# Embedding tower for 512 samples: a fourth fetch of table rows moves from GpSimd's gathers to single-row DMAs of SyncE and ScalarE

## The chip, the cores and the metric

One core of a Trainium2 chip. The metric is device time in microseconds (us) of one execution; the profile is of one execution, whose span begins with the first instruction.

## The reference

For each of 512 samples, 32 rows of 256 floats are looked up in 32 embedding tables (1000, 1250 or 12500 rows each), all dot products between different rows of a sample are taken, and a small MLP follows. Cut to what matters:

```python
e = jnp.stack([tbl_0[ids[:, 0]], ..., tbl_31[ids[:, 31]]], axis=1)   # 512 x 32 x 256
iu, ju = jnp.triu_indices(32, k=1)
z = jnp.einsum('bnd,bmd->bnm', e, e)[:, iu, ju]                       # 496 dots a sample
h = jnp.concatenate([z, dense_ctx], axis=1)                           # 16 dense inputs more
h = jnp.maximum(h @ W_top1 + b_top1, 0.0)                             # 512
h = jnp.maximum(h @ W_top2 + b_top2, 0.0)                             # 256
y = h @ W_top3                                                        # 1
```

All of it is float32.

## The kernel before

**Fetches.** A fetch brings 128 table rows of 1 KB, one for each partition: four samples by 32 fields (or 28 own fields and shared places for the others). There are 120 fetches, numbered 0 to 119 and taken in 60 pairs. Blocks of 128 samples have 32, 28, 28 and 32 fetches: in the two middle blocks, four fields of small tables are not fetched but looked up on TensorE with one-hot masks (`look_up`, L460 to L475, the products of L471; its eight units are copied out by ScalarE at L842, `copy_looked_up`).

**Three ways of fetching.** 117 fetches are indirect DMAs of GpSimd (`POOL` in the profile, L402), each into one of ten buffers (`rows`, `RING`); number n of this list waits until the fetch that held its buffer is transposed (L401). The three fetches in `SINGLE` (43, 83 and 109, L75) have a buffer of their own (`single_rows`) and are fetched row by row, 384 DMAs of 1 KB. The addresses of these rows are computed by VectorE in `row_at` (L654, L657). An engine that issues rows first loads 32 addresses into registers (one TENSOR_LOAD, L364) and then issues 32 DMAs (L369), inside `fetch_rows`. SyncE does nothing else between its first loads and the last store: it issues rows 0 to 319 in order as fast as it can (L379 to L381), that is fetch 43, fetch 83 and 64 rows of fetch 109. ScalarE issues rows 320 to 383 at the end of its program for each of the pairs 10 to 41, two rows a pair (`some_rows`, L832).

**TensorE.** For each pair p (L608 to L615): transposes both fetches of pair p (`transpose_fetch`, L420; the last fetch at L624), then takes the dots of pair p-1 (`gram_pair`, L435), then a part of a look-up, then pieces of the MLP (`MLP_AT`, L501, L578, L590) or, for the last block, of the MLP by sets of 32 samples (`SETS_AT`, L520, L530, L551). The order is written out by hand in these tables. After pair 58's turn come the dots of pair 58, the transposes of pair 59, its dots and the last two sets.

**VectorE** copies each transposed pair from PSUM (L337, L340), makes the masks (L672) and copies half of the dots to `z` (L321, L328). **ScalarE** copies the other half. In its turn for pair p it does, in this order: the MLP's activations, `copy_looked_up` if a unit ended with pair p-1, `place(p+1)` (L354: it puts the looked-up rows of pair p+1 beside the fetched ones, for which `gram_pair(p+1)` waits), dots, a piece of `move_dots` (L805: four small DMAs within SBUF for each block, which the first MLP product of the block waits for; those of block 0 in pairs 20 to 23, of block 1 in pairs 34 to 37), a load of a weight or table, and then its rows:

```python
place(pair + 1)
...
for b, n in MOVE_AT.get(pair, ()):
    move_dots(b, n)
load_at(pair)
some_rows(pair)
```

Of the kernel before, what the change touches and what calls it, by code (L numbers as in the profile page):

```python
# [71 lines left out]
MOVES = len(ALONE) + len(MOVED)  # L72


SINGLE = (43, 83, 109)  # L75
SP_ROWS = 320
ACT_ROWS = P * len(SINGLE) - SP_ROWS
ACT_ROW_PAIRS = range(10, 42)
LOAD = 32

GATHERED = tuple(n for n in range(FETCHES) if n not in SINGLE)

# [107 lines left out]
def tower_kernel(nc, ids, single_ids, hot_ids, hot_tables, tables, dense, w1, w1_packed, w2, vectors, tail, y):  # L190
    with ExitStack() as ctx:
        def sb(name, shape, dt=F32):
            return ctx.enter_context(nc.sbuf_tensor(name, shape, dt))
# [4 lines left out]
        def sem(name):  # L198
            return ctx.enter_context(nc.semaphore(name))
# [4 lines left out]
        rows = sb("rows", [P, RING, DIM])  # L204
        single_sb = sb("single_sb", [1, 2, SP_ROWS + ACT_ROWS], I32)
        row_at = sb("row_at", [1, SP_ROWS + ACT_ROWS], I32)
        single_rows = sb("single_rows", [P, len(SINGLE), DIM])
        hot_ids_sb = sb("hot_ids_sb", [P, BLOCKS - 1, HOT, BLOCK], I32)
# [73 lines left out]
        rows_landed = [sem(f"rows_landed_{n}") for n in range(RING)]  # L282
        single_landed = [sem(f"single_landed_{n}") for n in range(len(SINGLE))]
        transposed = sem("transposed")
# [77 lines left out]
        def fetch_rows(engine, kind, lo, hi):  # L362

            _, starts = nc.values_load_multi_w_load_instructions(  # L364
                row_at[:, lo:hi], engines=[kind], min_val=0, max_val=(tables.shape[0] - 1) * ROW_BYTES,
                skip_runtime_bounds_check_because="each DMA checks its own address against the table's end")
            for n, start in enumerate(starts):
                at, p = divmod(lo + n, P)
                yield engine.dma_start(single_u8[p:p + 1, at, :], tables_u8[bass.ds(start, ROW_BYTES)]  # L369
                                       ).then_inc(single_landed[at], 16)  # L370
# [4 lines left out]
        def _(sp):  # L375
            sp.dma_start(ids_sb[:], ids).then_inc(ids_loaded, 16)
            sp.dma_start(single_sb[:], single_ids).then_inc(single_loaded, 16)
            sp.wait_ge(row_at_ready, 1)
            for lo in range(0, SP_ROWS, LOAD):  # L379
                for _ in fetch_rows(sp, mybir.EngineType.SP, lo, min(lo + LOAD, SP_ROWS)):  # L380
                    pass  # L381
# [25 lines left out]
        def _(pe):  # L407
            def fetched(fetch):
                if fetch in SINGLE:
                    n = SINGLE.index(fetch)  # L410
                    pe.wait_ge(single_landed[n], 16 * P)
                    return single_rows[:, n, :]
                n = GATHERED.index(fetch)
                pe.wait_ge(rows_landed[n % RING], 16 * (n // RING + 1))
                return rows[:, n % RING, :]
# [351 lines left out]
        def _(act):  # L767
# [57 lines left out]
            def all_rows():  # L825
                for lo in range(SP_ROWS, SP_ROWS + ACT_ROWS, LOAD):
                    yield from fetch_rows(act, mybir.EngineType.Activation, lo,
                                          min(lo + LOAD, SP_ROWS + ACT_ROWS))

            rows_left = all_rows()  # L830

            def some_rows(pair):  # L832
                if pair in ACT_ROW_PAIRS:
                    if pair == ACT_ROW_PAIRS[0]:
                        act.wait_ge(row_at_ready, 1)
                    for _ in range(ACT_ROWS // len(ACT_ROW_PAIRS)):
                        next(rows_left)

            def copy_looked_up(unit):
                l, b = UNIT[unit]  # L840
# [52 lines left out]
            for pair in range(PAIRS - 1):  # L893
                mlp_behind(pair)
                for unit in range(UNITS):
                    if UNIT_END[unit] == pair - 1:
                        copy_looked_up(unit)
                place(pair + 1)
                if pair == 2:
                    act.wait_ge(vec_loaded, 16)  # L900
                for part, piece in DOTS_AT.get(pair, ()):
                    dots(part, piece)
# [4 lines that stand above are left out]
# [99 lines left out]
```

## Time and profile before

| | us |
|---|---|
| median of 3 runs | 164.48 |
| lowest and highest of them | 164.38, 165.02 |
| the profiled execution's own time | 165.76 |
| its span | 163.9 |

| engine | busy us | share | instructions |
|---|---|---|---|
| TensorE matmul (PE) | 141.8 | 87% | 3214 |
| VectorE (DVE) | 91.1 | 56% | 277 |
| ScalarE (ACT) | 46.5 | 28% | 143 |
| GpSimd (POOL) | 112.4 | 69% | 124 |

The span is shorter than the execution's own time by 1.9 us, which lies around it. Busy time leaves out DMA issues: the queue side of SyncE and ScalarE (SPq, ACTq) appears in the timeline only. ScalarE's queue side works ahead of its computing side by an instruction or so, so that a DMA issue can lie beside a copy.

### The profile page before, as it was taken

What the parts mean: (1) busy time and instruction counts of PE and PEld (TensorE: products, weight loads), DVE (VectorE), ACT (ScalarE), POOL (GpSimd) and SP (SyncE); (2) the same over time, 40 slices, a digit from 0 to 9 for tenths busy, and PEclk for the clock granted to TensorE, in tenths of its full rate; (3) what the DMA queues carried; (4) which work ended last, traced back from release to release, by engine and by line L of the source; (5) the groups of instructions that cost most, each with busy time, mean ns of one, the idle gap of its engine ahead of it and who ended that gap; (6) DMA issues with size and microseconds to landing.
All of it is one profiled execution on the core that took longest, in us unless ns stands there. A gap on an engine that the chain in (4) does not pass through costs nothing.

```text
span 163.9 us, 7924 instructions
## 1 busy us (share of the span) xinstructions
PE 141.8 (87%) x3214; PEld 121.3 (74%) x3214; DVE 91.1 (56%) x277; ACT 46.5 (28%) x143; POOL 112.4 (69%) x124
## 2 busy tenths in 40 slices
PE   6697994999999897499999977899895699999794
PEld 6595974888878776398988865589673598898583
DVE  2191333459936568039573974367865715737642
ACT  0003010134020631205351642056460502416240
POOL 3777777777777777777777777777777777775000
PEclk9999999699999999969999999699999569999999
DMA  1699689687945843446786844433434343334000
GB/s 34 140 311 337 191 254 291 235 247 219 279 153 118 271 119 107 112 120 183 219 233 190 244 113 126 123 105 105 116 118 118 104 121 110 100 106 116 14 4 5
DMA packets 11300, 25.44 MB, mean 155 GB/s; under 512 B 2958, under 2 KB 4574, under 8 KB 11264
## 3 DMA queue, kind: packets, MB, share of 16 engines
q0 software_dynamic: 5616, 15.34, 33.0%
q10 hardware_dynamic: 4860, 9.14, 17.4%
q1 hardware_dynamic: 788, 0.46, 1.0%
q8 instruction: 25, 0.41, 1.0%
q14 instruction: 11, 0.09, 0.2%
HBM read 24.71 MB, written 0.00 MB: 151 GB/s over the span
## 4 chain that ended last, share of the span: by engine, by line
PE 45%; DMA 25%; POOL 13%; DVE 7%; issue 6%; ACTq 2%; ACT 1%; POOLq 0%
DMA rows<-tables,idx 24%; POOL rows L402 13%; PE xt_ps L420 12%; PE hot_ps L471 11%; PE gram_ps L435 7%; PE act_ps L501 4%; PE hot_ps L520 3%; PE dve_ps L501 3%; DVE mask L672 2%; DVE xt L337 2%; DMA ids_sb<-ids 1%; PE gram_ps L520 1%; ACTq L805 1%; DVE z L321 1%; ACTq L369 1%
## 5 line engine op out<-in xcount | busy, mean ns | idle before, releaser
L402 POOL DMA_INDIRECT rows<-tables,idx x117 | 111.6, 954 | 37.2 <-issue 26.0
L420 PE MATMUL xt_ps<-ident,rows 128*128 128x128 f32 x232 | 41.3, 292 | 12.7 <-DMA rows<-tables,idx 12.4
L420 PEld LDWEIGHTS xt_ps<-ident,rows 128*128 128x128 f32 x232 | 28.1, 148 | 18.1 <-DMA rows<-tables,idx 16.7
L471 PE MATMUL hot_ps<-mask,hot_sb 128*128 128x128 f32 x256 | 37.7, 295 | 3.3 <-ACT hot_xt L842 3.1
L337 DVE COPY xt<-xt_ps 128x512 f32<-128x512 f32 (+1 forms) x32 | 21.8, 682 | 31.0 <-PE xt_ps L420 29.1
L471 PEld LDWEIGHTS hot_ps<-mask,hot_sb 128*128 128x128 f32 x256 | 32.3, 200 | 4.6 <-issue 3.5
L435 PEld LDWEIGHTS gram_ps<-xt 128*32 128x32 f32 x1920 | 22.1, 116 | 12.8 <-issue 10.3
L435 PE MATMUL gram_ps<-xt 128*32 128x32 f32 x1920 | 29.0, 203 | 1.5 <-DVE xt L337 1.0
L348 DVE COPY last_xt<-xt_ps 128x64 f32<-128x64 f32 x28 | 7.6, 271 | 23.9 <-PE xt_ps L420 23.2
L321 ACT COPY z<-gram_ps 32x128 f32<-32x128 f32 (+1 forms) x56 | 19.4, 347 | 4.7 <-PE gram_ps L435 3.8
L321 DVE COPY z<-gram_ps 32x128 f32<-32x128 f32 (+1 forms) x56 | 19.2, 343 | 0.9
L354 ACT COPY xt<-hot_xt 128x64 f32<-128x64 f32 x28 | 6.9, 245 | 38.6 <-PE gram_ps L435 34.9
L340 DVE COPY xt<-xt_ps 128x448 f32<-128x448 f32 x28 | 17.2, 615 | 0.0
L672 DVE TENSOR_SCALAR mask<-hot_ids_sb,hot_number 128x128 f32<-128x128 int32 x64 | 13.6, 309 | 0.0
L842 ACT COPY hot_xt<-hot_ps 128x256 f32<-128x256 f32 x8 | 5.0, 623 | 25.1 <-PE hot_ps L471 23.6
L328 ACT COPY z<-gram_ps 32x64 f32<-32x64 f32 (+1 forms) x32 | 8.7, 272 | 10.4 <-PE gram_ps L435 10.1
L479 PE MATMUL hot_ps<-ident 128*128 128x128 f32 x62 | 8.5, 304 | 1.6 <-POOL ident L392 1.6
L328 DVE COPY z<-gram_ps 32x64 f32<-32x64 f32 (+1 forms) x32 | 8.6, 269 | 1.5 <-PE gram_ps L435 1.1
L479 PEld LDWEIGHTS hot_ps<-ident 128*128 128x128 f32 x62 | 8.1, 160 | 1.6 <-POOL ident L392 1.6
L501 PE MATMUL act_ps<-z,w_packed_sb 128*128 128x128 f32 x48 | 8.3, 316 | 0.0
L501 PE MATMUL dve_ps<-z,w_packed_sb 128*128 128x128 f32 x48 | 7.6, 294 | 0.0
L501 PEld LDWEIGHTS act_ps<-z,w_packed_sb 128*128 128x128 f32 x48 | 6.9, 217 | 0.3
(70 smaller groups left out, 80.3 us busy)
## 6 DMA issues: line engine op xcount, KB each, us to landing
single_rows<-tables SPq DMA_DIRECT2D x320, 1.0 KB
hot_sb<-hot_tables ACTq DMA_DIRECT2D x8, 512.0 KB, 5.0
w_sb<-w ACTq DMA_DIRECT2D x8, 256.0 KB
rows<-tables,idx POOLq DMA_INDIRECT x117
w_packed_sb<-w_packed ACTq DMA_DIRECT2D x5, 256.0 KB
single_rows<-tables ACTq DMA_DIRECT2D x64, 1.0 KB
hot_ids_sb<-hot_ids ACTq DMA_DIRECT2D x2, 256.0 KB, 3.6
w_sb<-w ACTq DMA_DIRECT2D x1, 512.0 KB
```

The source lines that it names most:

```text
L321: last = copy(z_by_quad[FIELDS * jq:FIELDS * (jq + 1), q, first:end, :].rearrange("p g (h s) -> p g h s", s=FOURS), gram_ps[FIELDS * q:FIE ...
L328: last = copy(z_by_quad[FIELDS * jq:FIELDS * (jq + 1), q, first:end, lo:SLOTS], gram_ps[FIELDS * q:FIELDS * (q + 1), part % 3, 0:end - fir ...
L337: return copy(xt[:, bank, :, places].rearrange("p k l q f -> p k (l q f)"), xt_ps[:, bank, :, places].rearrange("p k l r -> p k (l r)"))
L340: return copy(xt[:, bank, :, places].rearrange("p k l q f -> p (k l) q f")[:, :, :, 0:COLD[b]], xt_ps[:, bank, :, places, 0:OWN[b]].rearra ...
L348: return copy(to[:, :, :, field:field + count].rearrange("p k s f -> p k f s"), ps)
L402: pool.indirect_dma_start(rows[:, n % RING, :], None, tables, bass.IndirectOffsetOnAxis(idx[:, fetch:fetch + 1], 0)).then_inc(rows_landed[ ...
L420: last = nc.tensor.transpose(xt_ps[:, fetch // 2 % 2, k, fetch % 2, :], x[:, P * k:P * (k + 1)], ident[:])
L435: last = nc.tensor.matmul(gram_ps[FIELDS * q:FIELDS * (q + 1), part % 3, at, :], x, x, start=(k == 0), stop=(k == CHUNKS - 1))
L471: last = nc.tensor.matmul(hot_ps[:, k, :], hot_sb[:, l, c, P * k:P * (k + 1)], mask[:, unit % MASKS, c, :], start=(c == 0), stop=(c == HOT ...
L479: nc.tensor.transpose(hot_ps[:, 0, :], ident[:], ident[:])
L501: last = nc.tensor.matmul(h1_ps[m], w1_packed_sb[:, s, P * m:P * (m + 1)], z[:, FOURS + s, samples] if s < FOURS else z_alone[:, samples], ...
L672: last = nc.vector.tensor_scalar(mask[:, unit % MASKS, c, :], hot_ids_sb[:, b, l, :], hot_number[:, c:c + 1], None, ALU.is_equal)
```

## The change

Four fetches go row by row, 43, 85, 117 and 113 in the order of the list, and 116 are gathered. Their 512 rows are divided so: SyncE issues rows 0 to 359, which are fetch 43, fetch 85 and 104 rows of fetch 117; ScalarE issues rows 360 to 511, the last 24 rows of fetch 117 and fetch 113. ScalarE issues four rows a pair (152 / 50 rounded up) from pair 4, so that its rows end with pair 41 as before. Its addresses begin at 360 x 4 = 1440 bytes, a multiple of 16.

```diff
-SINGLE = (43, 83, 109)
-SP_ROWS = 320
+SINGLE = (43, 85, 117, 113)
+SP_ROWS = 360
 ACT_ROWS = P * len(SINGLE) - SP_ROWS
-ACT_ROW_PAIRS = range(10, 42)
+ACT_ROW_PAIRS = range(4, 54)
 LOAD = 32
...
                 if pair in ACT_ROW_PAIRS:
                     if pair == ACT_ROW_PAIRS[0]:
                         act.wait_ge(row_at_ready, 1)
-                    for _ in range(ACT_ROWS // len(ACT_ROW_PAIRS)):
-                        next(rows_left)
+                    for _ in range(-(-ACT_ROWS // len(ACT_ROW_PAIRS))):
+                        next(rows_left, None)
```

On ScalarE, in the turns of pairs 19 to 22 (L805 is a move of dots, L369 a row, L364 a load of addresses, L842 the copy of a looked-up unit):

```order
 L354 COPY xt<-hot_xt 128x16x4
 L321 COPY z<-gram_ps 32x16x8 x2
 L805 DMA z_alone<-z 60x1x128
-L369 DMA single_rows<-tables 1x1024 x2
+L364 TENSOR_LOAD row_at
+L369 DMA single_rows<-tables 1x1024 x4
 L354 COPY xt<-hot_xt 128x16x4
 L805 DMA z_alone<-z 44x1x128
-L369 DMA single_rows<-tables 1x1024 x2
+L369 DMA single_rows<-tables 1x1024 x4
 L842 COPY hot_xt<-hot_ps 128x2x128
```

Between the first move of dots and the copy of the looked-up unit now stand a load of addresses and four rows more. ScalarE's loads stand in the turns of pairs 4, 12, 20, 28 and 36; before, in those of pairs 10 and 26.

On ScalarE, in the turns of pairs 35 to 37:

```order
 L354 COPY xt<-hot_xt 128x16x4
 L805 DMA z<-z 7x4x128
-L369 DMA single_rows<-tables 1x1024 x2
+L364 TENSOR_LOAD row_at
+L369 DMA single_rows<-tables 1x1024 x4
 L354 COPY xt<-hot_xt 128x16x4
 L805 DMA z<-z 3x4x128
```

Here the load stands ahead of the fourth move of block 1.

On SyncE, the end of its rows:

```order
 L364 TENSOR_LOAD row_at
 L369 DMA single_rows<-tables 1x1024 x32
+L364 TENSOR_LOAD row_at
+L369 DMA single_rows<-tables 1x1024 x32
+L364 TENSOR_LOAD row_at
+L369 DMA single_rows<-tables 1x1024 x8
 L383 DMA y<-y_row 1x512
```

Forty rows and two loads come behind the ten loads and 320 rows of before.

## Rows read from the trace of the kernel before

**Rows 1.** The page, costliest groups: GpSimd's gathers

```profile
L402 POOL DMA_INDIRECT rows<-tables,idx x117 | 111.6, 954 | 37.2 <-issue 26.0
```

**Rows 2.** Timeline of POOL: start us, us, engine line op, count, idle before

```profile
5.04 0.95 POOL L402 DMA_INDIRECT rows<-tables,idx  x1 [0.30 <-issue]
...
75.55 0.95 POOL L402 DMA_INDIRECT rows<-tables,idx  x1 [0.30 <-issue]
...
123.19 0.94 POOL L402 DMA_INDIRECT rows<-tables,idx  x1 [0.30 <-PE xt_ps L420]
...
149.51 0.95 POOL L402 DMA_INDIRECT rows<-tables,idx  x1 [0.30 <-issue]
```

**Rows 3.** Timeline of PE from 106 us: transposes of certain fetches, the work between

```profile
106.57 1.27 PE L501 MATMUL act_ps<-z,w_packed_sb 128*128 128x128 f32 x8
...
110.25 0.38 PE L420 MATMUL xt_ps<-ident,single_rows 128*128 128x128 f32 x2
...
126.07 0.44 PE L420 MATMUL xt_ps<-ident,rows 128*128 128x128 f32 x2 [0.86 <-DMA rows<-tables,idx]
...
128.24 1.12 PE L420 MATMUL xt_ps<-ident,rows 128*128 128x128 f32 x4 [1.34 <-DMA rows<-tables,idx]
...
135.14 0.60 PE L420 MATMUL xt_ps<-ident,rows 128*128 128x128 f32 x4
...
137.28 0.60 PE L420 MATMUL xt_ps<-ident,rows 128*128 128x128 f32 x4
...
150.92 0.60 PE L420 MATMUL xt_ps<-ident,rows 128*128 128x128 f32 x4
...
153.07 0.46 PE L435 MATMUL gram_ps<-xt 128*32 128x32 f32 x32 [0.20 <-DVE xt L337]
...
153.74 0.27 PE L624 MATMUL xt_ps<-ident,rows 128*128 128x128 f32 x1
```

**Rows 4.** What writes or reads row_at: duration ns min/median/max, first and last start

```profile
L364 SPq TENSOR_LOAD <-row_at x10: 2023/2124/2185, 4.2 to 120.9; - x10
L364 ACTq TENSOR_LOAD <-row_at x2: 2156/2169/2182, 35.0 to 78.1; - x2
L654 DVE CUSTOM_DVE_ANT_0 row_at<-single_sb x1: 540/540/540, 3.2 to 3.2; 1x768 uint16<-1x768 uint16 x1
L657 DVE TENSOR_SCALAR row_at<-row_at x1: 347/347/347, 3.8 to 3.8; 1x384 int32<-1x384 int32 x1
```

**Rows 5.** Line L369 on SyncE, 108 to 134 us (64 rows, one load between)

```profile
L369 SPq DMA_DIRECT2D single_rows<-tables x64: 227/228/445, 110.2 to 133.7; - x64
```

**Rows 6.** Line L369 on SyncE, 105 to 110 us: the last rows of fetch 83

```profile
L369 SPq DMA_DIRECT2D single_rows<-tables x10: 227/228/229, 104.9 to 107.7; - x10
```

**Rows 7.** Timeline of DVE: its copy of pair 58

```profile
152.33 0.69 DVE L337 COPY xt<-xt_ps 128x512 f32<-128x512 f32 x1
```

**Rows 8.** Timeline of ACT, 63 to 68 us: turns of pairs 20 to 22

```profile
63.57 1.04 ACTq L805 DMA_DIRECT2D z_alone<-z  x1
64.72 0.73 ACTq L369 DMA_DIRECT2D single_rows<-tables  x2
...
66.48 0.70 ACTq L369 DMA_DIRECT2D single_rows<-tables  x2
67.23 0.61 ACT L842 COPY hot_xt<-hot_ps 128x256 f32<-128x256 f32 x1 [1.44 <-issue]
```

**Rows 9.** Timeline of PE, 64 to 73 us

```profile
67.98 1.13 PE L471 MATMUL hot_ps<-mask,hot_sb 128*128 128x128 f32 x8 [3.14 <-ACT hot_xt L842]
...
72.05 0.92 PE L420 MATMUL xt_ps<-ident,rows 128*128 128x128 f32 x4
```

**Rows 10.** Timeline of ACT, 96 to 103 us: first and fourth move of block 1

```profile
96.53 0.95 ACTq L805 DMA_DIRECT2D z_alone<-z  x1
...
102.02 0.79 ACTq L805 DMA_DIRECT2D z<-z  x1
```

**Rows 11.** Stretches: us, busy (count) of PE, PEld, DVE, ACT, POOL, PEclk, DMA share, GB/s

```profile
128.20:134.10 5.90, 5.86 (x83) 5.03 (x84) 3.16 (x9) 2.16 (x8) 4.67 (x5) 0.50 0.40 111
134.10:140.00 5.90, 5.90 (x111) 5.31 (x114) 3.07 (x8) 1.80 (x7) 4.38 (x6) 1.00 0.37 103
```

## The prediction

> **What bounds the kernel now.** I read the page's costliest groups first. GpSimd issues 117 gathers of 954 ns [rows 1], and its timeline has them from 5.04 to 149.51 us at an even pace, 144.47 / 115 = 1.256 us each, with 0.30 us between two [rows 2]: GpSimd never waits for a buffer. Does TensorE wait for it? In TensorE's timeline the last wait for a gather ends at 128.24 us, with fetches 98 and 99 [rows 3]. From there on TensorE has work without a DMA wait up to the end. How close the gathers run I take from fetch 97: issued at 123.19, awaited by TensorE and transposed at 126.07, so a gather needs 2.88 us from the start of its issue [rows 2, 3]. The last one, issued at 149.51, is then there at 152.39, and TensorE transposes it at 153.74: 1.35 us to spare. So the kernel is bound by the gathers until fetch 99 and by TensorE, with VectorE's copies, after it. Earlier there is one stretch, from 64.8 to 67.98 us, where TensorE waits 3.14 us for ScalarE's copy of a looked-up unit [rows 9].
>
> **What the removed gather gives: 0.** Ahead of fetch 99 two fetches go row by row in either kernel (43 and 83, now 43 and 85), so fetch 99 is gather number 97 of the list in both and comes at the same time. Only behind fetch 117 is the list one gather shorter, and fetches 118 and 119 come 1.256 us earlier, where they already had 1.35 us to spare. Behind fetch 109, now gathered, fetches 110 to 112 come 1.256 us later, still covered by TensorE's own work; fetch 83, now gather number 82 (the one at 5.04 is number 1), is issued at 5.04 + 81 x 1.256 = 106.8 and needed at 110.25 [rows 3], which leaves 3.4 us against the 2.88 needed.
>
> **SyncE's forty rows more: the term that I expect to decide.** SyncE's loads of addresses start from 4.2 to 120.9, ten of them [rows 4], so a round of load and 32 rows takes 116.7 / 9 = 12.97 us. Nothing in its program waits. The eleventh load would start at 133.9 and the twelfth at 4.2 + 11 x 12.97 = 146.9. VectorE's two operations on the list grow by a third, (0.54 + 0.35) / 3 = 0.3 us [rows 4]: 147.2. This load fetches 8 addresses instead of 32. No row shows such a load; it costs between 0.5 us (a quarter of 2.12) and 2.12 us (the same). I take 1.2, between them, since nothing here tells a fixed part from one for each address. The Trainium skill speaks of it twice: "DMA: Bandwidth & Descriptors", section Latency and other measured facts, gives a load a floor of about 0.6 us, and "Runtime: NRT & Kernel Launch", section Instruction fetch mechanics, about 0.2 us a register. The second is contradicted here, since 32 addresses took 2.12 us and not 6.4. By the floor of 0.6 us an estimate with the rest in proportion would be 1.0 us, and the sum 0.2 us less.
>
> A row takes (133.7 - 110.2 - 2.0) / 63 = 0.34 us [rows 5, 4]. The eighth row starts 7 x 0.34 = 2.4 us after the load: 147.2 + 1.2 + 2.4 = 150.8. The landing of a row has no time of its own in the answers. From above: the last row of fetch 83 starts at 107.7 [rows 6], and the fetch is transposed at 110.25 without a wait, so at most 2.55 us. From below I take half a gather's time, 1.4 us. I take 2.0, so fetch 117 is complete at 152.8. Before, pair 58 (fetches 116 and 117) was transposed in 0.60 us from 150.92, fetch 117 from about 151.2 [rows 3]. So TensorE waits **1.6 us** for it.
>
> Who waits behind this? TensorE stands ahead of the dots of pair 57, of a set's second layer and of the dots of pair 58, and it issues them all before the transposes of pair 59. Before, this work stood between 151.2 and 153.07 and ended in a wait of only 0.20 us for VectorE's copy of pair 58 [rows 3, 7]. VectorE would copy pair 58 from 153.1 instead of 152.33 and be done ahead of TensorE. So 0.2 us at most of the 1.6 us is taken up; everything behind is a chain to the end. The term: **+1.4 to +1.6 us**. Its ends: with the load at 0.5 and landing at 1.4, 151.5, +0.3; with 2.12 and 2.55, 154.3, and 0.3 more for SyncE's queue slowed by ScalarE's rows, +3.4.
>
> **ScalarE's rows and loads.** It issues 88 rows more, at 0.33 to 0.36 us (0.73 for two, [rows 8]), and three loads of 2.17 us more [rows 4]. In most turns this lies beside ScalarE's idle time (46.5 us busy of 163.9). Two places are not covered:
>
> - Pairs 20 to 22. The chain of waits goes through ScalarE here: move 63.57, rows 64.72, move, rows 66.48, copy of the unit 67.23, for which TensorE waits until 67.98 [rows 8, 9]. The load now stands in it, and four rows more: 2.17 + 4 x 0.35 = 3.6 us. The next unit's copy (pair 26) gets two rows more ahead of it, 0.7 us. TensorE is 3.6 to 4.3 us late. What is late next is GpSimd: the gather of fetch 58, at 75.55, waits for fetch 48, transposed between 72.05 and 72.97 in its pair [rows 2, 9], so it has about 2.9 us. GpSimd stops for the remaining 0.7 to 1.4 us, and the gathers, which bound the kernel until fetch 99, come later by that. I take 1.0. TensorE's other 3 us are given back in the waits for gathers that follow.
> - Pairs 34 to 37. The four moves of block 1 run from 96.53 to 102.81 one behind the other [rows 10], and TensorE begins the block's MLP, which needs the fourth, at 106.57 [rows 3]. Now six rows (2.1 us) and a load (2.17) more stand ahead of the fourth move: 4.3 us, of which 106.57 - 102.81 = 3.8 less the move's landing (at least 1.4) is covered. TensorE waits some 1.9 us there, more if ScalarE is late already. The waits for gathers that follow up to 128.24, of which 0.86 and 1.34 are shown [rows 3], take that up.
>
> The 1.0 us does not add to SyncE's term: TensorE reaches fetch 117 1.0 us later and then waits 0.6 us for it rather than 1.6. The end is set by the later of the two, SyncE's.
>
> **Sum.** Span 163.9 + 1.5 = 165.4; with the 1.9 us around it this profiled execution would take 167.3. It is 1.28 us longer than the median of the runs, 164.48, against which I state the forecast: 164.48 + 1.5 = **166.0 us**. A measurement of this kernel tells about 0.5% from no change, 0.8 us: 163.7 to 165.3.
>
> **Rivals.**
>
> - *ScalarE's waits outweigh SyncE's rows.* TensorE enters the third block several us late: 4 us from pair 22, of which the waits before pair 39 give back only a part, then ScalarE's turns of pairs 34 to 37, which follow TensorE's dots and so are late too, add to it. If it is more than the waits up to fetch 99 hold, it goes to the end. For it speaks that each piece stands in ScalarE's order; against, that the gathers' waits are frequent. It gives 2.5 to 4 us: 167 to 168.5. Chance 0.22.
> - *All is hidden: no change.* SyncE's last row lands within 0.8 us of TensorE's need and the gathers lose less than 0.8 us. It needs the short load, 0.5 us, and the quick landing. 164.5 to 165.3. Chance 0.14, and 0.05 of my forecast's own range falls here too.
> - *Faster, by the clock.* TensorE's granted clock was 0.50 (1.2 GHz) from 128.2 to 134.1 and 1.00 (2.4 GHz) behind it [rows 11], after the short waits for gathers that end at 128.24. Two pairs took 135.14 - 128.24 = 6.9 us there, the next one 2.14 [rows 3]: the low clock cost 6.9 - 4.3 = 2.6 us. A TensorE that comes late to these fetches doesn't wait for them and may keep 2.4 GHz. The Trainium skill says that the default is the throttled state and that activity releases it ("TensorE: Matmul & The Clock Gate", Part 1: The HAM clock gate); the trace agrees, the low clock follows 0.86 and 1.34 us of waits. It decides only if SyncE's last row is there before 151.2 as well, for which its rounds would have to be 0.15 us shorter each than measured; against it speaks that they were even. The time would be 164.48 - 2.6 = 161.9. Chance 0.09.
>
> The change does what it says: the order of the instructions shows 116 gathers and the rows where the text has them.
>
> **Numbers.** My forecast, SyncE's last rows: 0.55, range 164.8 to 167.9. Slower by over 0.5%: 0.55 + 0.22 - 0.05 = 0.72; within: 0.14 + 0.05 = 0.19; faster: 0.09. The range 164.6 to 168.2 leaves out the faster case, about half of the case without change, and the upper end of the first rival.
>
> **What would show it.** SyncE's last row starts at 150.8 (150 to 152); its last load, how long 8 addresses take. TensorE's transpose of fetch 117 has a wait of 0.6 to 1.6 us, ended by single_rows, where there was none. TensorE's wait for the copy at L842 near 65 us grows from 3.1 to 6.7 us. GpSimd's timeline has a gap over 0.30 us near 76 us, of 0.7 to 1.4 us. The granted clock behind 128 us tells the last rival. I am wrong if the transpose of fetch 117 has no wait, or if GpSimd is never held up.

## The result and the profile after

| | before | the changed kernel |
|---|---|---|
| median, us | 165.16 (164.38 to 166.47, 6 runs) | 177.42 (176.0 to 179.09, 6 runs) |
| profiled execution: own time, span | 165.76, 163.9 | 177.47, 175.6 |

The changed kernel is slower: ratio 1.0713, 95% interval 1.0666 to 1.0760, that is 12 us. Predicted were 166.0 us and a range of 164.6 to 168.2. The direction was right, the size was not. In some executions a kernel takes over 1.5% longer than its fastest one (179.09 us here): the medians in this text count them, the ratios leave them out.

The page of the changed kernel, the busy engines and the chain of waits (the chain that ended last, in shares of the span by engine and by line):

```profile
PE 140.9 (80%) x3214; PEld 121.7 (69%) x3214; DVE 91.0 (52%) x277; ACT 46.1 (26%) x143; POOL 111.2 (63%) x123
...
PE 42%; DMA 19%; ACTq 13%; POOL 9%; DVE 7%; issue 6%; ACT 2%
DMA rows<-tables,idx 15%; PE xt_ps L420 9%; POOL rows L402 9%; PE hot_ps L471 8%; PE gram_ps L435 8%; ACTq L369 6%; PE act_ps L501 5%; PE dve_ps L501 5%; ACTq L805 4%; DMA z<-z 3%; ACTq L364 3%; PE hot_ps L520 2%; DVE z L328 2%; DVE z L321 2%; DVE xt L337 1%
...
L402 POOL DMA_INDIRECT rows<-tables,idx x116 | 110.4, 952 | 44.2 <-issue 25.3
```

TensorE works as long as before (140.9 us against 141.8), in a span that is 11.7 us longer: the time went into its waits. The queue side of ScalarE is 13% of the chain, where it was 2%: its rows (L369) 6%, its moves (L805) 4%, its loads of addresses (L364) 3%. GpSimd idles 44.2 us instead of 37.2 [rows 1].

TensorE's timeline of the changed kernel from 64 us, the rows that hold its waits and the transpose of fetch 117 (idle time and what ended it in brackets):

```profile
64.45 0.38 PE L420 MATMUL xt_ps<-ident,single_rows 128*128 128x128 f32 x2
...
74.38 2.05 PE L471 MATMUL hot_ps<-mask,hot_sb 128*128 128x128 f32 x8 [7.00 <-ACT hot_xt L842]
...
84.91 1.35 PE L471 MATMUL hot_ps<-mask,hot_sb 128*128 128x128 f32 x10 [1.12 <-ACT hot_xt L842]
...
102.23 0.46 PE L435 MATMUL gram_ps<-xt 128*32 128x32 f32 x32 [0.64 <-ACT xt L354]
...
108.87 0.46 PE L435 MATMUL gram_ps<-xt 128*32 128x32 f32 x32 [1.49 <-ACT xt L354]
...
111.17 0.46 PE L435 MATMUL gram_ps<-xt 128*32 128x32 f32 x32 [1.25 <-DVE xt L340]
...
115.71 0.66 PE L435 MATMUL gram_ps<-xt 128*32 128x32 f32 x32 [3.03 <-issue]
...
119.09 2.05 PE L501 MATMUL act_ps<-z,w_packed_sb 128*128 128x128 f32 x8 [2.72 <-DMA z<-z]
...
162.97 0.38 PE L420 MATMUL xt_ps<-ident,single_rows 128*128 128x128 f32 x2
```

Two places stand out. At pair 22 TensorE waits 7.00 us for the copy of the looked-up unit, where it waited 3.14 [rows 9]. Between 101 and 119 us it waits six times (the five rows here and one of 0.21), 9.34 us in all: for ScalarE's copies (L354), once for VectorE's, 3.03 us that the profile puts down to nothing, and at last for the fourth move of block 1 (`z<-z`). There is no wait for a gather after 62.5 us; before, the last ended at 128.24 [rows 3]. And fetch 117, on which the forecast rested, is transposed at 162.97 without any wait.

How late TensorE is, from the start of the transpose of certain fetches in both traces (us):

| fetch | before | changed | later by |
|---|---|---|---|
| 42, ahead of the first place | 61.56 | 64.23 | 2.7 |
| 46, behind it | 68.94 | 76.22 | 7.3 |
| 74, ahead of the second place | 99.85 | 106.78 | 6.9 |
| 84, behind it | 112.17 | 126.16 | 14.0 |
| 98, the last that was waited for before | 128.24 | 139.00 | 10.8 |
| 117 | 151.14 | 162.97 | 11.8 |

Behind 64 us the kernel before waits eight times for gathers, 6.35 us in all, and the changed kernel never: that much of the lateness was taken up, 2.8 us within the second place and the rest between fetches 84 and 98.

What ScalarE does in the second place, from the chain of waits between 105 and 120 us (start, us, what; the first of the four rows stands for each group of rows):

```profile
105.65 0.96 ACTq L805
...
106.71 0.38 ACTq L369
...
108.16 0.24 ACT xt L354
108.41 0.63 ACTq L805
...
110.62 0.40 ACTq L805
...
111.48 2.27 ACTq L364
...
115.39 3.57 DMA z<-z
```

From 105.65 to 115.39 nearly each piece is an instruction of ScalarE's, one behind the other, with the load of addresses in the middle; then the fourth move takes 3.57 us from its issue to its landing, and TensorE goes on at 119.09. The 3.03 us ahead of 115.71 belong, as far as the times tell, to ScalarE's copy behind the load and four rows, which ends at 115.61:

```profile
115.37 0.24 ACT L354 COPY xt<-hot_xt 128x64 f32<-128x64 f32 x1 [4.34 <-issue]
```

The first and fourth move stood 5.5 us apart before (96.53, 102.02, [rows 10]) and 9.7 us now.

GpSimd's timeline at the first place:

```profile
77.12 0.94 POOL L402 DMA_INDIRECT rows<-tables,idx  x1 [4.52 <-PE xt_ps L420]
```

GpSimd stands idle 4.52 us instead of 0.30, until a buffer is free, and issues fetch 56 4.1 us later than before (73.04). The loads of addresses (all queues, duration ns min/median/max) and SyncE's last rows, 148 to 170 us:

```profile
L364 SPq TENSOR_LOAD <-row_at x12: 797/2129/2166, 4.3 to 147.4; - x12
L364 ACTq TENSOR_LOAD <-row_at x5: 2142/2170/2501, 21.0 to 111.5; - x5
```

```profile
L369 SPq DMA_DIRECT2D single_rows<-tables x8: 228/228/272, 148.3 to 150.6; - x8
```

Two stretches of the changed kernel, in the columns of [rows 11] (the third figure from the end is TensorE's granted clock). Behind the wait of 7.00 us the clock is at 0.51, and the eight products of pair 22 take 2.05 us instead of 1.13; from 128.2 to 134.1 it is at 1.00, where it was at 0.50:

```profile
74.30:78.30 4.00, 3.92 (x46) 3.56 (x47) 0.76 (x2) 0.24 (x1) 0.94 (x1) 0.51 0.04 8
128.20:134.10 5.90, 5.79 (x192) 5.05 (x191) 4.52 (x15) 4.02 (x16) 3.92 (x6) 1.00 0.33 96
```

### The profile page after: what moved, and what is told of

It is laid out like the page before. It is cut to its first block, busy times and chain, and to the rows that moved or that the text cites. A ratio compares the mean times of both kernels' runs of the same rounds, so it can differ in the third digit from the quotient of the medians.

```text
span 175.6 us, 8184 instructions
## 1 busy us (share of the span) xinstructions
PE 140.9 (80%) x3214; PEld 121.7 (69%) x3214; DVE 91.0 (52%) x277; ACT 46.1 (26%) x143; POOL 111.2 (63%) x123
## 4 chain that ended last, share of the span: by engine, by line
PE 42%; DMA 19%; ACTq 13%; POOL 9%; DVE 7%; issue 6%; ACT 2%
DMA rows<-tables,idx 15%; PE xt_ps L420 9%; POOL rows L402 9%; PE hot_ps L471 8%; PE gram_ps L435 8%; ACTq L369 6%; PE act_ps L501 5%; PE dve_ps L501 5%; ACTq L805 4%; DMA z<-z 3%; ACTq L364 3%; PE hot_ps L520 2%; DVE z L328 2%; DVE z L321 2%; DVE xt L337 1%
## 5 line engine op out<-in xcount | busy, mean ns | idle before, releaser
L402 POOL DMA_INDIRECT rows<-tables,idx x116 | 110.4, 952 | 44.2 <-issue 25.3
L420 PE MATMUL xt_ps<-ident,rows 128*128 128x128 f32 x230 | 39.6, 287 | 8.6 <-DMA rows<-tables,idx 8.6
L471 PE MATMUL hot_ps<-mask,hot_sb 128*128 128x128 f32 x256 | 36.9, 291 | 8.5 <-ACT hot_xt L842 8.5
L471 PEld LDWEIGHTS hot_ps<-mask,hot_sb 128*128 128x128 f32 x256 | 31.7, 196 | 9.9 <-issue 8.7
L420 PEld LDWEIGHTS xt_ps<-ident,rows 128*128 128x128 f32 x230 | 27.3, 146 | 12.9 <-DMA rows<-tables,idx 11.6
L354 ACT COPY xt<-hot_xt 128x64 f32<-128x64 f32 x28 | 6.8, 245 | 42.3 <-PE gram_ps L435 24.8
L842 ACT COPY hot_xt<-hot_ps 128x256 f32<-128x256 f32 x8 | 5.0, 625 | 32.0 <-PE hot_ps L471 17.2
L479 PE MATMUL hot_ps<-ident 128*128 128x128 f32 x62 | 9.5, 328 | 1.6 <-POOL ident L392 1.6
L479 PEld LDWEIGHTS hot_ps<-ident 128*128 128x128 f32 x62 | 9.1, 174 | 1.6 <-POOL ident L392 1.6
```

Of the source, the lines that this page charges most:

```text
L402: pool.indirect_dma_start(rows[:, n % RING, :], None, tables, bass.IndirectOffsetOnAxis(idx[:, fetch:fetch + 1], 0)).then_inc(rows_landed[ ...
L420: last = nc.tensor.transpose(xt_ps[:, fetch // 2 % 2, k, fetch % 2, :], x[:, P * k:P * (k + 1)], ident[:])
L471: last = nc.tensor.matmul(hot_ps[:, k, :], hot_sb[:, l, c, P * k:P * (k + 1)], mask[:, unit % MASKS, c, :], start=(c == 0), stop=(c == HOT ...
L479: nc.tensor.transpose(hot_ps[:, 0, :], ident[:], ident[:])
```

## The experiments

The chips on which they ran are of two sorts, and the numbers can't be understood without that. On two chips the kernel before takes 165 us as in the first profile; on three others it takes 232 us, in all of its runs there. The change costs 4% on the 232 us chips and 7% in the measurement above, where the kernel before takes 165 us; the changed kernel itself was not run again on a 165 us chip. So each result is a ratio to the kernel before on the same chip, with its 95% interval, and the sort is named: a 165 us chip or a 232 us chip.

### The rows out of the turns that TensorE waits for

The changed kernel with ScalarE's rows kept out of the turns of pairs 20, 21 and 34 to 37:

```diff
-ACT_ROW_PAIRS = range(4, 54)
+ACT_ROW_PAIRS = tuple(n for n in range(4, 60) if n not in (20, 21, 34, 35, 36, 37))
```

> The changed kernel with no rows in ScalarE's turns of pairs 20, 21 and 34 to 37 (they go four a pair in 4 to 19, 22 to 33 and 38 to 47): the same number of rows and loads, none among the moves of dots that TensorE waits for. Theory A and B agree that most of the 12 us goes: 166 to 168 us. With those stalls gone, SyncE's last rows come into view: theory C (the prediction's term) has TensorE wait 1 to 2 us for fetch 117; if TensorE is still 2 to 3 us late there for another reason, no such wait is seen. Rival D (rows cost wherever they are issued, through the DMA engines): 171 us or more.

> The same edit as e4_skip (no rows of ScalarE in the turns of pairs 20, 21 and 34 to 37, the changed kernel otherwise), on a chip where the kernel before takes about 165 us. Theory A (ScalarE's rows and loads among the moves are the cost): 166 to 169 us. Rival D (the rows cost wherever they are issued): 172 us or more. Theory C (SyncE's last rows): TensorE waits for fetch 117.

Measured, both on 232 us chips: 1.0117 (1.0048 to 1.0187) and 1.0102 (1.0064 to 1.0141). Of the wait at pair 22 1.95 us are left, which the profile puts down to nothing it shows; one of 2.19 us stands at pair 26, as in the changed kernel on such a chip (2.19 too; 1.54 in the variant without fetch 117, below). With the turn of pair 25 free as well, on a 165 us chip:

```diff
+ACT_ROW_PAIRS = tuple(range(4, 20)) + (22, 23, 24) + tuple(range(26, 34)) + tuple(range(38, 49))
```

> The changed kernel with ScalarE's rows kept out of the same turns, four a pair in 4 to 19, 22 to 24, 26 to 33 and 38 to 48. Against the variant with the turns of 20, 21, 34 to 37 free (ratio 1.010) it also spares the turn of pair 25. Theory A: its wait of 2.2 us at pair 26 shrinks to 0.8 or less, ratio 0.995 to 1.003. Rival D (the 88 rows more cost something everywhere): 1.008 or more.

Measured: 168.08 us against 165.41, ratio 1.012 (1.0057 to 1.0182). Same rows, same loads, same gathers, same 40 rows of SyncE: 10 of the 12 us are gone by the place of ScalarE's rows alone. The rest is what rival D had, 1.008 or more; theory A's 0.995 to 1.003 is missed, and so is its 0.8 us for the wait at pair 26. TensorE's timeline of this kernel, the rows of pairs 22 and 26, the beginning of the MLP of block 1, and the last wait for a gather:

```profile
68.14 1.60 PE L471 MATMUL hot_ps<-mask,hot_sb 128*128 128x128 f32 x8 [1.53 <-ACT hot_xt L842]
...
78.78 1.35 PE L471 MATMUL hot_ps<-mask,hot_sb 128*128 128x128 f32 x10 [1.43 <-ACT hot_xt L842]
...
107.91 1.13 PE L501 MATMUL act_ps<-z,w_packed_sb 128*128 128x128 f32 x8 [0.99 <-DMA z<-z]
...
128.89 0.44 PE L420 MATMUL xt_ps<-ident,rows 128*128 128x128 f32 x2 [1.27 <-DMA rows<-tables,idx]
```

7.00 us have become 1.53, the 9.34 us in the middle 2.69 (0.99 here, 1.17 and 0.53 in pairs ahead of it), and TensorE waits for gathers again, for fetch 99 until 128.89 us. Fetch 117 is transposed at 153.1, and there is no wait for it, though SyncE's last row starts at 151.6:

```profile
L369 SPq DMA_DIRECT2D single_rows<-tables x6: 228/228/228, 150.0 to 151.6; - x6
L420 PEld LDWEIGHTS xt_ps<-ident,single_rows x2: 140/140/141, 153.0 to 153.2; 128*128 128x128 f32 x2
```

So this row landed within 1.5 us of its start; the forecast had 2.0. TensorE comes 2.0 us later here than in the kernel before. There it came at 151.14, and at that time the last row was not even issued here: with a TensorE on time there would have been a wait.

### One of the two places alone

The changed kernel with the turns of 34 to 37 free, and those of 20 and 21 as they are, on a 165 us chip:

```diff
+ACT_ROW_PAIRS = tuple(n for n in range(4, 54) if n not in (34, 35, 36, 37))
```

> The changed kernel with no rows or load of ScalarE in the turns of pairs 34 to 37 alone; the turns of 20 and 21, with their load, as in the changed kernel. If the two stalls add up: the stall of 112 to 119 us goes and with it about 6 us, 170 to 172 us. Rival F (what the first stall leaves late is given back by the waits for gathers once the second is gone): 166 to 168 us.

Measured: 172.18 us against 165.12, ratio 1.0387 (1.0312 to 1.0461). Its timeline of TensorE:

```profile
73.61 2.05 PE L471 MATMUL hot_ps<-mask,hot_sb 128*128 128x128 f32 x8 [6.97 <-ACT hot_xt L842]
...
112.25 1.13 PE L501 MATMUL act_ps<-z,w_packed_sb 128*128 128x128 f32 x8 [0.20 <-DMA z<-z]
...
134.10 0.69 PE L420 MATMUL xt_ps<-ident,rows 128*128 128x128 f32 x2 [2.10 <-DMA rows<-tables,idx]
```

The first wait is untouched, 6.97 us, and the wait for the fourth move is 0.20. From 1.071 to 1.039, 5.3 us, is what the turns of 34 to 37 cost; from 1.039 to 1.012, some 4.4 us, the turns of 20, 21 and 25. The stalls add up, as the first theory had it. Of the 7.1 us that TensorE is late at fetch 76 here (108.24; 101.13 before), 5.5 are left at fetch 117 (156.69; 151.14), although it waits for gathers again in block 3: the gathers are late themselves. GpSimd is held at fetch 56 here too (issued at 76.36) and issues fetch 99 at 129.93, 4.2 us later than before (125.69).

### A load of addresses, or four rows?

The kernel before with ScalarE's 64 rows from pair 20 on, so that its two loads stand in the turns of 20 and 36; nothing is added, but its rows go on to pair 51 and so through the turns of 45 and 46, where block 2's dots are moved and no row stood before:

```diff
-ACT_ROW_PAIRS = range(10, 42)
+ACT_ROW_PAIRS = range(20, 52)
```

> The kernel before, three fetches by row and 117 gathers, with ScalarE's two rows a pair moved from pairs 10 to 41 to pairs 20 to 51: its two loads of addresses then stand in the turns of pairs 20 and 36, where the changed kernel has its third and fifth; no instruction is added. Theory A: slower by 3 to 6 us, TensorE's wait for the looked-up copy 5.3 us instead of 3.1. Rival B: within 1 us of the kernel before.

> The same edit as e2_loads (the kernel before with ScalarE's two loads in the turns of pairs 20 and 36, two rows a pair from 20 to 51). Theory A1: 3 to 6 us slower than before, 168 to 171. Rival B: within 1 us of it.

> The same edit as e2_loads (the kernel before, ScalarE's two loads in the turns of pairs 20 and 36, two rows a pair), on a chip that takes 165 us for the kernel before. On the slow chips TensorE's wait at pair 22 was 6.45 us, 3.2 more than without the load. Expected here: 5.5 to 6.5 us of wait at pair 22, and 3 to 6 us in all; if the waits for gathers give all of it back, under 1 us.

Measured: 1.0174 (1.0097 to 1.0250) and 1.0158 (1.0105 to 1.0211) on 232 us chips, and 169.29 us against 165.12 on a 165 us chip, ratio 1.023 (1.0179 to 1.0280), 3.8 us. Instructions that were all there before cost 3.8 us by the turn they stand in, within theory A's 3 to 6. On the 165 us chip, TensorE's timeline of pair 22 and of the MLP of blocks 1 and 2:

```profile
69.91 2.05 PE L471 MATMUL hot_ps<-mask,hot_sb 128*128 128x128 f32 x8 [6.37 <-ACT hot_xt L842]
...
109.42 2.04 PE L501 MATMUL act_ps<-z,w_packed_sb 128*128 128x128 f32 x8 [1.50 <-DMA z<-z]
...
134.08 1.13 PE L501 MATMUL act_ps<-z,w_packed_sb 128*128 128x128 f32 x8 [2.50 <-DMA z<-z]
```

The 3.8 us are not the two loads alone. Against the trace of the kernel before on a 165 us chip, fetch 46 is transposed 2.8 us later, fetch 84, behind the second load, 5.2, but fetch 98 only 1.7: the waits for gathers took up 3.5 us. Fetch 117 is 3.5 us late, and 1.8 of them come behind fetch 98, where TensorE waits 2.50 us for the moves of block 2, whose turns have rows now. What the loads alone cost was not separated from that.

The kernel before with four rows, and no load, in the turns of the moves:

```diff
+ACT_ROW_PAIRS = tuple(range(12, 32)) + (34, 35, 36, 37)
...
-                    for _ in range(ACT_ROWS // len(ACT_ROW_PAIRS)):
+                    for _ in range(4 if pair in (20, 21, 22, 23, 34, 35, 36, 37) else 2):
```

> The kernel before with ScalarE's 64 rows dealt out otherwise: two a pair in the turns of pairs 12 to 19 and 24 to 31, four in 20 to 23 and 34 to 37, loads of addresses at 12 and 24. Four rows in the turns of the moves and no load among them, no row more in all. Theory B (the rows among the moves are a cost of their own): 2 to 4 us slower than before. Theory A1 (the loads are the cost, not the rows): within 1 us of it.

Measured, on a 232 us chip: 1.0153 (1.0088 to 1.0217), 3.5 us. That is theory B's figure, but the trace doesn't bear out its reason. Beside the variant without fetch 117 on such a chip, TensorE is 0.4 us later at fetch 50, behind the first moves; it is 3.4 us later at fetch 56 and no later than that behind the second moves (1.5 at fetch 80). The 3 us come at pairs 26 and 27, where TensorE's clock is at half. The products of pair 26 take 2.47 us instead of 1.35. The stretch from 108.9 to 115.8 us, first with the four rows, then without fetch 117:

```profile
108.90:115.80 6.90, 5.73 (x55) 5.37 (x56) 1.80 (x5) 1.88 (x5) 2.28 (x4) 0.51 0.39 120
```

```profile
108.90:115.80 6.90, 6.38 (x107) 5.87 (x108) 2.44 (x8) 2.19 (x7) 3.44 (x4) 1.00 0.46 151
```

Whether the rows brought the low clock there is not shown. So this run says how long TensorE waits at pair 22, not what four rows a turn cost. And the changed kernel itself there:

> The changed kernel itself, beside the kernel before on the same chip, since the chips of the other experiments take 232 us for the kernel before. Theory A (turns of ScalarE among the moves): still clearly slower than before, and slower than the variant with rows from pair 8 (ratio 1.03) and than the one with empty turns (1.01): 1.045 to 1.075. Rival E (on a chip this slow the waits are hidden): within 1% of the variant from pair 8.

Measured: 1.0408 (1.0341 to 1.0475), within 1% of the variant from pair 8 (1.0358 on this chip): rival E's figure, so the 232 us chips can't tell these two apart.

TensorE's wait at pair 22 on the 232 us chips puts the two side by side: 3.25 us with rows as before (and 116 gathers; the kernel before has no trace on such a chip, and on the 165 us chips 3.16 with 117 and 3.18 with 116), 4.49 with four rows in each turn, 6.45 with the load, 7.43 in the changed kernel with both. Here are the rows of these four kernels, in that order:

```profile
94.68 2.04 PE L475 MATMUL hot_ps<-mask,hot_sb 128*128 128x128 f32 x8 [3.25 <-ACT hot_xt L847]
```

```profile
95.20 1.90 PE L471 MATMUL hot_ps<-mask,hot_sb 128*128 128x128 f32 x8 [4.49 <-ACT hot_xt L842]
```

```profile
97.17 2.04 PE L471 MATMUL hot_ps<-mask,hot_sb 128*128 128x128 f32 x8 [6.45 <-ACT hot_xt L842]
```

```profile
99.27 2.05 PE L471 MATMUL hot_ps<-mask,hot_sb 128*128 128x128 f32 x8 [7.43 <-ACT hot_xt L842]
```

Four rows for two in the two turns ahead of the copy are 4 x 0.33 = 1.3 us and show as 1.24; the load shows as 3.2, and both together as 4.2. In the kernel with the load and no more rows the load took 2.18 us, but the move ahead of it 1.52 instead of 1.05. On the 165 us chips the wait is 3.16 us in the kernel before, 4.52 with four rows in each turn (next section), 7.00 with the load as well: 1.36 for the rows, 2.48 for a load that took 2.50 there. Neither of the theories is right alone: as a wait at pair 22, the load and the rows cost about what they take, both of them.

### The loads moved away, the rows left

The changed kernel with rows from pair 8, so that its loads stand at 8, 16, 24, 32 and 40:

```diff
-ACT_ROW_PAIRS = range(4, 54)
+ACT_ROW_PAIRS = range(8, 58)
```

> The changed kernel with ScalarE's rows started at pair 8 instead of 4, still four a pair: its five loads of addresses fall on the turns of pairs 8, 16, 24, 32 and 40 and no longer on 20 and 36, between moves of dots. Theory A (a load of addresses among the moves is the main cost): TensorE's wait for the copy of the looked-up unit near 70 us falls from 7.0 to about 4.8 us, the stall near 112 to 119 us from 5.8 to about 2, and the time to about 170 us. Rival B (the four rows a pair on ScalarE are the cost, wherever the loads stand): 174 us or more.

> The same edit as e1_start8 (the changed kernel with ScalarE's rows from pair 8, so loads at 8, 16, 24, 32, 40 and not at 20 and 36). Theory A1 (the loads among the moves): 170 to 172 us. Rival B (four rows in each of these turns do it): 174 us or more.

> The same edit as e1_start8 (the changed kernel with rows from pair 8, no load among the moves, four rows in each of these turns), on a chip that takes 165 us for the kernel before. Loads the main cost: 168 to 171 us. Four rows a turn the main cost: 173 us or more.

Measured: 1.0358 (1.0287 to 1.0429) and 1.0317 (1.0260 to 1.0375) on 232 us chips, slightly less than the changed kernel. On a 165 us chip: 182.35 us against 165.12, ratio **1.1002** (1.0934 to 1.1070), more than the changed kernel. The figure for the loads failed; the one for four rows (173 us or more) held, but says nothing of a time above the changed kernel's. TensorE's timeline:

```profile
58.91 1.13 PE L471 MATMUL hot_ps<-mask,hot_sb 128*128 128x128 f32 x8 [2.83 <-ACT hot_xt L842]
...
72.91 2.05 PE L471 MATMUL hot_ps<-mask,hot_sb 128*128 128x128 f32 x8 [4.52 <-ACT hot_xt L842]
86.11 1.35 PE L471 MATMUL hot_ps<-mask,hot_sb 128*128 128x128 f32 x10 [3.51 <-ACT hot_xt L842]
...
121.01 1.42 PE L501 MATMUL act_ps<-z,w_packed_sb 128*128 128x128 f32 x8 [3.03 <-DMA z<-z]
...
145.67 2.05 PE L501 MATMUL act_ps<-z,w_packed_sb 128*128 128x128 f32 x8 [2.74 <-DMA z<-z]
```

The wait at pair 22 is down from 7.0 to 4.5 us as expected, but the loads, now in the turns of 16 and 24, stand ahead of the next copies that TensorE awaits, at pair 18 (2.83 us, where the changed kernel has 0.37) and at pair 26 (3.51 instead of 1.12); and with rows until pair 45 the moves of block 2, in the turns of 45 and 46, are late too (2.74 instead of 0.67). So "a load among the moves" was too narrow. In these two traces the loads in the turns of 16, 20, 24 and 36 are each followed by such a wait, and those of 4, 8, 12, 28 and 40 are not. The clock has a part too: its mean was 0.933 here and 0.951 in the changed kernel, which makes some 24 us of the span at half clock (1.2 GHz) instead of 17 (an estimate from the means).

### The removed gather alone

The kernel before with fetch 117 left out: 116 gathers, its buffer set to zero, no row more.

```diff
-SINGLE = (43, 83, 109)
+SINGLE = (43, 83, 109, 117)
+BY_ROW = SINGLE[:3]
...
-ACT_ROWS = P * len(SINGLE) - SP_ROWS
+ACT_ROWS = P * len(BY_ROW) - SP_ROWS
```

> The kernel before with fetch 117 left out (its buffer holds zeros), so 116 gathers, and no row more on SyncE or ScalarE: what the removed gather is worth by itself. The prediction's step (nothing waits for the last gathers): within 0.5 us of the kernel before, 165. Rival (each gather less is worth its 1.26 us of GpSimd): 164 or less.

> The same edit as e3_gather (the kernel before with fetch 117 left out, its buffer zeros, 116 gathers), on a chip that takes 165 us for the kernel before. The prediction's step: within 0.5 us of the kernel before. Rival: 1.0 to 1.3 us faster.

Measured: 0.9973 (0.9924 to 1.0021) on a 232 us chip; 165.58 us against 165.12 on a 165 us chip, ratio 1.0007 (0.9964 to 1.0051). The gather that the change saves is worth nothing that can be measured, as the prediction had it.

### The same turns freed in the kernel before

The kernel before with its 64 rows out of the turns of 20, 21, 25 and 34 to 37, and the kernel before itself for a trace, on the same chip:

```diff
+ACT_ROW_PAIRS = tuple(range(10, 20)) + (22, 23, 24) + tuple(range(26, 34)) + tuple(range(38, 49))
```

> The kernel before with ScalarE's 64 rows kept out of the turns of pairs 20, 21, 34 to 37 (moves of dots) and 25 (ahead of a unit's copy), two a pair in 10 to 19, 22 to 24, 26 to 33 and 38 to 48. Theory A (a row or load of ScalarE ahead of a copy that TensorE awaits is paid in full): TensorE's wait at pair 22, 3.25 us in the kernel before on such a chip, nearly goes, and the kernel is 1 to 3 us faster than before. Rival: the wait is only moved to the gathers, no change.

> The kernel before itself, for its trace on such a chip: where the 67 us come from that it takes more here than in the first profile. By the traces of the experiments: TensorE pauses of about 0.5 us inside the dots, in every pair, with no wait that another engine ends, and GpSimd held up by its buffers from the first block on.

Measured, on a 165 us chip: 165.48 against 165.41, ratio 1.0002 (0.9963 to 1.0041). The rival was right. The kernel before waits 3.16 us at pair 22 there too; in the other kernel 1.51 us of it are left, and TensorE waits for gathers instead, five times between 90 and 97 us, 3.65 us in all. From TensorE's timeline, the kernel with free turns first, then the kernel before:

```profile
65.75 1.13 PE L471 MATMUL hot_ps<-mask,hot_sb 128*128 128x128 f32 x8 [1.51 <-issue]
...
90.40 0.44 PE L420 MATMUL xt_ps<-ident,rows 128*128 128x128 f32 x2 [0.69 <-DMA rows<-tables,idx]
...
94.10 0.44 PE L420 MATMUL xt_ps<-ident,rows 128*128 128x128 f32 x2 [1.51 <-DMA rows<-tables,idx]
```

```profile
67.09 2.05 PE L471 MATMUL hot_ps<-mask,hot_sb 128*128 128x128 f32 x8 [3.16 <-ACT hot_xt L842]
...
103.03 0.44 PE L420 MATMUL xt_ps<-ident,rows 128*128 128x128 f32 x2 [1.66 <-DMA rows<-tables,idx]
```

So 1.65 us of the wait at pair 22 cost the kernel before nothing, since the gathers set the pace; the changed kernel asks for more than that. I ran no version that is faster than the kernel before.

The expectation of the run for a trace was written before its chip was known; it drew a 165 us chip, so that how the 232 us arise is seen only in the experiments' traces (last section).

### What stayed open

The changed kernel with ScalarE's rows out of the turns of 45 and 46 too, in which the dots of block 2 are moved; and the kernel before with 40 rows of fetch 117 on SyncE alone (its other 88 rows are left out, zeros; 116 gathers):

```diff
+ACT_ROW_PAIRS = tuple(range(4, 20)) + (22, 23, 24) + tuple(range(26, 34)) + tuple(range(38, 45))
...
+                    for _ in range(5 if pair < 20 else 4):
```

```diff
+MORE = 40
...
+            for lo in range(SP_ROWS + ACT_ROWS, SP_ROWS + ACT_ROWS + MORE, LOAD):
+                for _ in fetch_rows(sp, mybir.EngineType.SP, lo, min(lo + LOAD, SP_ROWS + ACT_ROWS + MORE)):
+                    pass
```

> The changed kernel with ScalarE's 152 rows out of all turns of moves (20, 21, 34 to 37, 45, 46) and of 25: five a pair in 4 to 19, four in 22 to 24, 26 to 33 and 38 to 44. If the rest of the cost was the rows at 45 and 46: ratio 1.000 to 1.005, with TensorE then waiting 0.5 to 1.5 us for fetch 117 (SyncE's last row landed at 152.9 us in the variant before this one). If the 88 rows more cost by themselves: 1.01 or more.

> The kernel before with 116 gathers, where SyncE fetches 40 rows of fetch 117 behind its 320 (two loads and 40 rows more) and the other 88 rows of it are left out (zeros); ScalarE as before. The prediction's own term by itself: SyncE's last row lands at 151.8 to 152.8 us, TensorE waits 0.6 to 1.6 us for it, 0.4 to 1.5 us slower than before. Rival: TensorE is a little later there than in the first profile and nothing is seen, within 0.3 us.

Both drew a 232 us chip. The first: 1.0124 (1.0073 to 1.0176). That is the figure for "the 88 rows more cost by themselves", but it decides nothing, by a slip of mine: with five rows a pair a load falls ahead of the last row of pair 16's turn, shortly ahead of a unit's copy, and TensorE waits 3.90 us for that copy at pair 18 (2.22 with four rows a pair). The second: 1.0018 (0.9987 to 1.0049), no difference; but TensorE comes to fetch 117 at 217.9 on this chip, long after SyncE's last row, which starts at 170.9. So SyncE's term by itself, and the last 1.2% of the changed kernel with free turns, stay open.

## Why the prediction was wrong

- **The removed gather gives 0.** Right, by two runs.
- **SyncE's forty rows, the term that was to decide (+1.4 to +1.6 us).** The times of issue held: the twelfth load started at 147.4 (147.2 predicted) and took 0.80 us (1.2 taken, between 0.5 and 2.1); the last row started at 150.6 (150.8). The floor of 0.6 us that the Trainium skill gives ("DMA: Bandwidth & Descriptors", Latency and other measured facts) does not contradict the 0.80 us, and the estimate of 1.0 made from it was nearer than my 1.2. The landing was taken as 2.0 us; it was under 1.5 in the variant with free turns, by which the wait would have been 0.9 us at most (150.6 + 1.5 against 151.2). But it did not happen, since TensorE was 11.8 us late at fetch 117. As a cost of the change the term measured 0.
- **ScalarE, pairs 20 to 22: TensorE 3.6 to 4.3 us late.** This is the first step that failed. The wait itself was right: predicted to grow from 3.1 to 6.7 us, it was 7.00. But TensorE was 7.3 us late behind it. 2.7 us it had brought along (fetch 42), which the prediction puts at nothing: it had waited 7.4 us for gathers up to 48 us instead of 5.3, although GpSimd issued them at the same times. 3.9 us is the wait's growth, and about 0.9 us the products behind it at the low clock. The variants with rows from pair 4 on are 2 us late at pair 15 (49.5, 49.1, 49.0 us, against 47.1 and 46.8 in the two traces of the kernel before and 48.3 with rows from pair 8); whether by the rows' own DMAs or by the table loads beside them was not separated.
- **GpSimd held for 0.7 to 1.4 us, I take 1.0.** It was held 4.1 us longer than the usual 0.30, and fetch 98 is issued 7.0 us later than before. The room of 2.9 us was right (7.3 less 4.1 is 3.2); what was wrong is the lateness that it was taken from.
- **ScalarE, pairs 34 to 37: 1.9 us.** The second step that failed, and the larger one. Measured: 9.34 us of waits, less the 2.8 us that TensorE had waited for gathers in this stretch before; the run that frees these turns puts the cost at 5.3 us. I had priced the load and six rows against the slack of 3.8 us, taking 1.4 us for the landing of the fourth move; it took 3.57 from its issue to its landing, 2.8 behind its 0.8 us on the queue. And I had priced only this one wait, not the copies (L354) of the same turns, which stand behind the same rows and load: 0.64, 0.21, 1.49 and, by the times, 3.03 us.
- **"Given back in the waits for gathers that follow."** This happened, and was not enough. The kernel before had 6.35 us of such waits behind 64 us, and they are all gone. 3.6 us at the first place and 1.9 at the second are less than they hold; 7.3 us and 9.34 us are 10 us more, and that went to the end. The prediction did not add up what its waits could hold. In the changed kernel the late gathers play no part, since TensorE never waits for one there; with the second place free (172.18 us) they do.
- **The sum.** I took the later of two ends, SyncE's, with 1.0 us for ScalarE. ScalarE's two places set the end and added up: 4.4 and 5.3 us by the runs, and some 2 us that stay when the turns are free and that no run explains. The rival of ScalarE's waits had the right mechanism and places; its 2.5 to 4 us were short by a factor of three, by the same two sizes.
- **The clock.** The rival that was faster by the clock had one thing right: TensorE comes late to the fetches at 128 us, does not wait, and keeps the full clock there. But the low clock came in other places, around the waits that end at 74.4 and 119.1 us (0.51 from 74.3 to 78.3, 0.55 from 115.0 to 122.6). In all it is the same: the mean granted clock was 0.951 against 0.948 before.

## What to carry to other kernels

Where an in-order engine stands between two stages, price each instruction added to its queue at its full duration until the next thing that the bound engine awaits from it, and look in every turn for all the things that it awaits, not for the last one only; instructions that issue or load nothing big (0.33 us a row, 2.15 us a load) are no cheaper than copies there. Idle time of the bound engine takes up lateness, but no more than its sum from there to the end (6.35 us here), and less when what it waits for is late too: count the buffers between the two (2.9 us of room here). Add the lateness of all places before setting it against that sum. Busy time of the middle engine (26% here) says nothing about either.

## What was not expected of the hardware

- Kernels that are the same take 165 us on two of the chips and 232 us on three others, and most of the difference lies inside TensorE's stream. The waits of TensorE's weight loads of the dots, in the kernel before on a 165 us chip and in the variant without fetch 117 on a 232 us chip (us in total, times, longest):

```profile
PEld gram_ps L435 <- issue: 10.5, 58, 0.3
```

```profile
PEld gram_ps L439 <- issue: 59.8, 136, 2.0
```

  "Issue" is time in which it waited for nothing that the profile shows; its growth is 49 of the 66 us between the two spans (164.1 and 229.7). The mean granted clock is lower too, 0.889 against 0.948, which makes some 51 us at half clock instead of 17 (an estimate from the means). With TensorE this slow the second stall of the changed kernel is hidden: it is 7.1 us later than the variant without fetch 117 at fetch 68 and 7.2 at fetch 80. The ratio falls from 1.07 to 1.04. Why these chips pause, no run here shows.
- A load of 32 addresses from SBUF takes 2.1 us and one of 8 takes 0.80: about 0.055 us an address on top of 0.36 us. ScalarE's last load, of 24, fits (1.66 to 1.74 us in the variants of the changed kernel; the line gives 1.68). The Trainium skill has about 0.2 us a register ("Runtime: NRT & Kernel Launch", Instruction fetch mechanics), where it speaks of loads from HBM; for these loads the measurement decides.
- ScalarE's load right behind a move is not always 2.15 us: 2.50 in the turn of pair 20 of the changed kernel, 2.66 in the turn of pair 36 of the variant with two rows a pair from 20, but 2.19 in the turn of pair 20 there, where the move ahead took 1.56 us instead of 1.05. What makes it longer, no run here separates.
